# Graph attention on one core: the first row group's second edges as float8, half of each packed exponential and of each normalised row by ScalarE

## The chip, the cores and the metric

The kernel runs on one core of a Trainium2 chip. The metric is device time in microseconds, the median of three runs. The engines are called as in the profile: PE (TensorE, PEld its weight loads), DVE (VectorE), ACT (ScalarE), POOL (GpSimd), SP (SyncE, which issues DMAs). A q behind a name is the engine's queue of DMA issues.

## The reference

One graph attention layer with a residual, on 8192 nodes of 128 features:

```python
h = jnp.maximum(_layernorm(x, axis=-1), 0.0)          # x: (8192, 128) float32
Wh = h @ W                                            # W: (128, 128)
f1, f2 = Wh @ a[:128, 0], Wh @ a[128:, 0]
e = leaky_relu(f1[:, None] + f2[None, :], 0.2)
e = where(adj == 0, -inf, e)                          # adj: (8192, 8192) int32 of 0 and 1
out = x + softmax(e, axis=1) @ Wh
```

## The kernel before

The adjacency matrix is 256 MB of int32, and every entry is read once. Its rows are worked in 16 row groups of 512 rows (four rows to a partition). A row group goes over 16 units of 512 columns, that is 512 nodes. For each unit the entries of the four rows (0 or 1 each, as bytes) are added up into one code per word, PE transposes the codes, ACT unpacks them into marks (`unpack` in the first row group, `take` and `part` later), DVE makes four tiles of weights from the marks and the exponentials of the nodes (`weights`, L987), and PE multiplies these with the nodes' features, high and low halves in float16 (`product`, L476 and L480), into four accumulators. A unit is 16 pairs of such products.

The first row group is the one that matters here. While it runs, the kernel also computes what all row groups need, one group of 512 nodes per unit: the statistics of x on DVE (`statistics`, L913; `inverses` for a batch of groups, with a root by ACT, L776 and L779), the normalised x (`normalise`, into the tile `xn`: one row of four by ACT, L635, three by POOL, L283), its transposes on PE (`x_transposes`, L422) and the relu by ACT (L643), the features on PE (`features`, L440), their copy to SBUF by ACT (`keep`, L649), two small exponentials by ACT (`exponentials`, L675 and L676), their packing into two float16 halves of one word by DVE (`pack`, L965 and L966), the scaled features by POOL (`scaled`, L330), and their high and low float16 parts by ACT and DVE (`high_part`, L764; `low_part`, L974, which ends in `pair_ready`, for which PE waits before it starts a unit).

The order on each engine is written out by hand: each engine walks its own list of these steps and waits on semaphores. In unit b of the first group PE does the first four products' pairs, `features(b+2, 0)`, `x_transposes(b+3)`, four more pairs, `features(b+2, 1)`, four more, the transposes of the codes of unit b+2, and the last four. `x_transposes(g)` waits for ACT's part of `xn` (`xn_ready`) and for POOL's (`xn_pool`). ACT does `high_part(b+1)`, `keep(b+2, 0)`, in some units a root, `second`, `relu(b+3)`, `keep(b+2, 1)`, `exponentials(b+2)`, `unpack(b+2)`, `normalise(b+4)`. POOL does `mix(b+2)`, `normalise(b+4)`, `scaled(b+2)` and then issues loads. DVE does the weights of unit b+1, in some units with `inverses` between their halves (units 2, 5 and 9 among them), `low_part(b+1)`, `pack(b+2)` and the statistics of further groups (`STATS`; group 10 in the loop's third round).

The adjacency of the first row group is loaded by POOL's queue in 16 parts of one unit each (`load_part`, L256; four rows of 512 entries per partition, converted from int32 to bytes on the way), ten of them before POOL's other work and six later (`EARLY`, `PARTS`). The later row groups are loaded in half chunks of two rows of 2048 entries per partition (`load_half`, L291), one half of them to bytes and the other to float8, in which a 1 is the byte 60. For the first group, where all four rows come as plain bytes, ACT multiplies rows 2 and 3 by 200 instead (`second`, L702) before POOL adds them to rows 0 and 1 (`mix`, L274).

x comes by SP's queue in six loads (`LOADS`): groups 0, 1, 2 to 3, 4 to 5, 6 to 9 and 10 to 15, called loads 0 to 5 here. The last three wait until parts 0, 1 and 3 of the adjacency have landed.

## Time and profile before

| | us |
|---|---|
| median of 3 runs (772.83, 772.83, 774.3) | 772.83 |
| the profiled execution | 773.42 |
| its span, first to last instruction | 771.5 |
| PE busy in it | 751.3 (97%) |
| DVE busy in it | 726.5 (94%) |
| ACT busy in it | 579.2 (75%) |
| POOL busy in it | 442.9 (57%) |

The profile is one execution, and all starts and durations below are of it. The busy shares are means over the first row group (up to about 88 us) and the fifteen others, which have different limits, so a change in the first row group is read from that stretch. A timeline row gives the start, the time from the first to the last instruction of the entry, the engine, the line, and in brackets the idle time of the engine before it with what released it.

### The profile page before, as it was taken

What the parts mean: (1) busy time and instruction counts of PE and PEld (TensorE: products, weight loads), DVE (VectorE), ACT (ScalarE), POOL (GpSimd) and SP (SyncE); (2) the same over time, 40 slices, a digit from 0 to 9 for tenths busy, and PEclk for the clock granted to TensorE, in tenths of its full rate; (3) what the DMA queues carried; (4) which work ended last, traced back from release to release, by engine and by line L of the source; (5) the groups of instructions that cost most, each with busy time, mean ns of one, the idle gap of its engine ahead of it and who ended that gap; (6) DMA issues with size and microseconds to landing.
All of it is one profiled execution on the core that took longest, in us unless ns stands there. A gap on an engine that the chain in (4) does not pass through costs nothing.

```text
span 771.5 us, 23891 instructions
## 1 busy us (share of the span) xinstructions
PE 751.3 (97%) x8676; PEld 687.7 (89%) x8676; DVE 726.5 (94%) x1183; ACT 579.2 (75%) x1139; POOL 442.9 (57%) x501
## 2 busy tenths in 40 slices
PE   6899899999999999999999999999999999999997
PEld 5789789999999999999999999999999999999986
DVE  6998899999999999999999999999999999999996
ACT  5889887777778777777877777777777777777762
POOL 8787865646646664664666456465655646564510
PEclk9999999999999999999999999999999999999999
DMA  9999899999999999999999999999999999997100
GB/s 171 179 105 108 85 114 128 108 114 120 107 126 100 116 93 113 108 100 114 97 121 94 118 97 99 112 104 121 90 120 93 99 111 102 115 97 82 19 15 18
DMA packets 48246, 79.70 MB, mean 103 GB/s; under 512 B 2834, under 2 KB 11732, under 8 KB 48212
## 3 DMA queue, kind: packets, MB, share of 16 engines
q0 software_dynamic: 41088, 67.12, 90.5%
q1 hardware_dynamic: 6976, 12.09, 4.6%
q8 instruction: 17, 0.28, 0.1%
q14 instruction: 17, 0.14, 0.1%
q10 hardware_dynamic: 148, 0.07, 0.0%
HBM read 276.37 MB, written 4.23 MB: 364 GB/s over the span
## 4 chain that ended last, share of the span: by engine, by line
PE 91%; DVE 4%; ACT 2%; DMA 1%; POOL 1%; issue 1%; DVEq 0%; ACTq 0%; POOLq 0%
PE acc L476 56%; PE acc L480 29%; PE stage L467 4%; DVE wt_ring L987 2%; PE stage L440 1%; DMA masks<-in_adj_dram 1%; DVE pairs L974 1%; PE stage L422 0%; ACT marks L727 0%; DVE stats L913 0%; PE stage L458 0%; POOL tmp L330 0%; POOL masks L274 0%; DVE xm L1082 0%; ACT wh L649 0%
## 5 line engine op out<-in xcount | busy, mean ns | idle before, releaser
L476 PE MATMUL acc<-pairs,wt_ring 128*128 128x258 f16 x4096 | 717.5, 274 | 4.9 <-DVE pairs L974 3.5
L987 DVE SCALAR_TENSOR_TENSOR wt_ring<-stage,packed,marks 128x512 f32<-128x512 f32 x1024 | 688.4, 744 | 30.9 <-PE acc L480 21.5
L480 PE MATMUL acc<-pairs,wt_ring 128*128 128x129 f16 x4096 | 697.7, 220 | 0.0
L476 PEld LDWEIGHTS acc<-pairs,wt_ring 128*128 128x128 f16 x4096 | 398.8, 98 | 56.2 <-DVE pairs L974 5.1
L480 PEld LDWEIGHTS acc<-pairs,wt_ring 128*128 128x128 f16 x4096 | 400.3, 98 | 4.9
L727 ACT ACTIVATE marks<-codes 128x512 uint16<-128x512 uint8 x480 | 274.6, 620 | 12.5
L717 ACT ACTIVATE codes<-stage 128x512 uint16<-128x512 uint8 x240 | 142.8, 595 | 147.1 <-PE stage L467 146.6
L291 POOL DMA_DIRECT2D masks<-in_adj_dram x120 | 87.7, 731 | 219.8 <-PE stage L467 198.9
L310 POOL TENSOR_TENSOR masks<-masks 128x512 int32<-128x512 int32 x120 | 150.6, 1282 | 1.3
L319 POOL TENSOR_TENSOR masks<-masks 128x256 int32<-128x256 int32 x120 | 87.6, 735 | 55.7 <-ACT masks L710 54.8
L710 ACT ACTIVATE masks<-masks 128x512 uint16<-128x512 uint16 x120 | 74.8, 623 | 1.3 <-POOL masks L310 0.7
L467 PE MATMUL stage<-ident,masks 128*128 128x128 f32 x240 | 67.0, 279 | 0.8 <-ACT codes L717 0.4
L467 PEld LDWEIGHTS stage<-ident,masks 128*128 128x128 f32 x240 | 33.7, 141 | 5.0 <-issue 1.5
L337 POOL TENSOR_SCALAR fin<-fin 128x516 f32<-128x516 f32 x15 | 22.8, 1519 | 2.1 <-ACT fin L752 1.6
L330 POOL TENSOR_TENSOR tmp<-wh,tmp 128x512 f32<-128x512 f32 x16 | 18.0, 1124 | 10.0 <-ACT tmp L676 10.0
L440 PE MATMUL stage<-wx,ht 128*128 128x130 f32 x120 | 20.9, 299 | 1.5 <-ACT ht L643 0.7
L283 POOL TENSOR_SCALAR xn<-xm,small 128x128 f32<-128x128 f32 x42 | 19.4, 471 | 4.3 <-DVE small L937 4.3
L752 ACT ACTIVATE fin<-acc 128x258 f32<-128x258 f32 x60 | 19.4, 381 | 0.0
L347 POOL TENSOR_TENSOR xm<-fin,xm 128x512 f32<-128x512 f32 x15 | 18.0, 1199 | 1.8 <-ACT fin L758 1.5
L758 ACT ACTIVATE fin<-fin,inv 128x128 f32<-128x128 f32 x60 | 19.0, 392 | 0.0
L440 PEld LDWEIGHTS stage<-wx,ht 128*128 128x128 f32 x120 | 16.6, 200 | 2.7 <-ACT ht L643 1.1
L685 ACT ACTIVATE marks<-stage 128x1024 uint16<-128x1024 uint8 x16 | 16.3, 1019 | 1.4 <-PE stage L458 1.4
(78 smaller groups left out, 201.3 us busy)
## 6 DMA issues: line engine op xcount, KB each, us to landing
masks<-in_adj_dram POOLq DMA_DIRECT2D x120, 512.0 KB, 9.7
masks<-in_adj_dram POOLq DMA_DIRECT2D x16, 256.0 KB, 21.9
out_dram<-xm SPq DMA_DIRECT2D x15, 256.0 KB, 7.8
ht<-e_words SPq DMA_DIRECT2D x14, 256.0 KB, 8.5
xm<-in_x_dram SPq DMA_DIRECT2D x1, 1536.0 KB, 13.4
xm<-in_x_dram SPq DMA_DIRECT2D x2, 512.0 KB, 6.6
xm<-in_x_dram SPq DMA_DIRECT2D x1, 1024.0 KB, 9.8
xm<-in_x_dram SPq DMA_DIRECT2D x2, 256.0 KB, 3.1
```

The costliest lines, as they stand in the source:

```text
L291: nc.gpsimd.dma_start(to[:, c * PACK + h:(c + 1) * PACK:2, :], adj_half[q, c, :, h::2, :]).then_inc(adj_second[c] if h else adj_loaded[c], 16)
L310: nc.gpsimd.tensor_tensor(edges4[:, c, :, 0, sl], edges4[:, c, :, 0, sl], edges4[:, c, :, 1, sl], ALU.add).then_inc(s["mixed4"], 1)
L319: nc.gpsimd.tensor_tensor(edges4[:, c, 0, 0, sl], edges4[:, c, 0, 0, sl], edges4[:, c, 1, 0, sl], ALU.add).then_inc(s["joined"], 1)
L337: nc.gpsimd.tensor_scalar(fin[:, :, E1:2 * E1], fin[:, :, E1:2 * E1], 1.0 / LOW, None, ALU.mult).then_inc(s["lows_scaled"], 1)
L440: mm = nc.tensor.matmul(to[:, r * 256:r * 256 + WC], ht[:, g % 2, k:k + P], wx[:], start=(r == 0), stop=(r == 1), skip_group_check=True)
L467: nc.tensor.transpose(stage[:, 0, 0:P], words[:, c * PACK, kk * P:(kk + 1) * P], ident[:]).then_inc(s["transposed"], 1)
L476: return nc.tensor.matmul(acc[:, r, 0:2 * E1], wtv[:, w, r, 1, :], pairv[:, t, :, 0:E1], start=st, stop=end)
L480: return nc.tensor.matmul(acc[:, r, E1:2 * E1], wtv[:, w, r, 0, :], pairv[:, t, 0, 0:E1], start=False, stop=False)
L710: nc.scalar.activation(twos[:, c, 1, 0, sl], twos[:, c, 1, 0, sl], ACT.Copy, scale=2.0).then_inc(s["doubled"], 1)
L717: nc.scalar.activation(codes2[:, b % 2, :].rearrange("p (s w) -> p s w", s=PACK), stage[:, 0, 0:P].bitcast(U8).rearrange("p (w s) -> p s w ...
L727: mm = nc.scalar.activation(split[:, b % MR, :].rearrange("p (s a w) -> p a s w", s=PACK, a=2)[:, h], codes[:, b % 2, :].rearrange("p (s w ...
L987: nc.vector.scalar_tensor_tensor(out=wtq[:, t % NW], in0=e_row, scalar=packed[:, t, 1:2], in1=edges[:, k], op0=ALU.max, op1=ALU.min).then_ ...
```

## The change

Rows 2 and 3 of the first row group are now loaded as float8, so that a 1 arrives as the byte 60, and `second` is gone; `mix` waits for the load alone, and `unpack` scales by 256/60. Each part of the load becomes two transfers, one for rows 0 and 1 and one for rows 2 and 3, on one semaphore that counts to 32. Parts 0 and 1 are still one unit each; the other seven are two units each, with 1024 entries to a row, so that there are 18 transfers in place of 16. Five parts are issued before POOL's other work, one after `scaled(1)`, and one each in the loop's first three rounds. SP's loads 3, 4 and 5 of x now wait for parts 0, 1 and 2, the last of which holds units 2 and 3.

The upper half of the packed exponential, which DVE made from the exponential by a multiplication, is now a third exponential of ACT with another bias, written as float16 between the two others; its constant is a fourth entry of `cst`, and `CUT` is 2 to the power of -16 lower.

ACT now normalises two rows of each group in place of one, and POOL two in place of three; `xn_ready` comes with ACT's second row.

```diff
-CUT = 1.0 - 2.0 ** -11
+CUT = 1.0 - 2.0 ** -11 - 2.0 ** -16
-SECOND = 200.0
-SPLIT = 256.0 / SECOND
+ONE8 = 60.0
+SPLIT = 256.0 / ONE8
-    EARLY = 10
+    EARLY = 5
-    PARTS = {0: (12,), 1: (13,), 2: (14, 15)}
+    PARTS = {0: (6,), 1: (7,), 2: (8,)}
+    UNITS = [(0, 1), (1, 2)] + [(u, u + 2) for u in range(2, UN, 2)]
...
-            for k, part in ((3, 0), (4, 1), (5, 3)):
-                sp.wait_ge(first_loaded[part], 16)
+            for k, part in ((3, 0), (4, 1), (5, 2)):
+                sp.wait_ge(first_loaded[part], 32)
                 load_x(k)
...
-            def load_part(u):
-                c, k = u // KC, u % KC
-                nc.gpsimd.dma_start(masks[:, c * PACK:(c + 1) * PACK, k * BANK:(k + 1) * BANK],
-                                    adj_first[0, u]).then_inc(first_loaded[u], 16)
+            def load_part(k):
+                lo, hi = UNITS[k]
+                c = lo // KC
+                at, to = (lo - c * KC) * BANK, (hi - c * KC) * BANK
+                for h, tiles in ((0, masks), (1, masks8)):
+                    sl = slice(HALF * h, HALF * (h + 1))
+                    nc.gpsimd.dma_start(tiles[:, c * PACK + HALF * h:c * PACK + HALF * (h + 1), at:to],
+                                        adj_first[0, :, sl, lo * BANK:hi * BANK]).then_inc(first_loaded[k], 16)
 
             load_part(0)
-            load_part(1)
...
-            for u in range(2, EARLY):
-                load_part(u)
+            for k in range(1, EARLY):
+                load_part(k)
...
-                pool.wait_ge(first_loaded[u], 16)
-                pool.wait_ge(s["second_ready"], u + 1)
+                pool.wait_ge(first_loaded[part_of(u)], 32)
...
-                for r in range(1, PACK):
+                for r in range(HALF, PACK):
...
             load_part(EARLY)
-            load_part(EARLY + 1)
...
-                for u in PARTS.get(b, ()):
-                    load_part(u)
+                for k in PARTS.get(b, ()):
+                    load_part(k)
...
-                t = g * PACK
-                nc.scalar.activation(xn[:, g % 2, 0:P], xm[:, g, 0:P], ACT.Identity, scale=small[:, 5, t:t + 1],
-                                     bias=small[:, 6, t:t + 1]).then_inc(s["xn_ready"], 1)
+                for r in range(HALF):
+                    t = g * PACK + r
+                    mm = nc.scalar.activation(xn[:, g % 2, r * P:(r + 1) * P], xm[:, g, r * P:(r + 1) * P],
+                                              ACT.Identity, scale=small[:, 5, t:t + 1], bias=small[:, 6, t:t + 1])
+                mm.then_inc(s["xn_ready"], 1)
...
                 nc.scalar.activation(exps, wh[:, sl, Fo:WC], ACT.Exp, scale=1.0 - SLOPE, bias=cst[:, 0:1])
+                nc.scalar.activation(packedv[:, sl, :, 1], wh[:, sl, Fo:WC], ACT.Exp, scale=1.0 - SLOPE,
+                                     bias=cst[:, 3:4])
...
-            def second(b):
-
-                c, k = b // KC, b % KC
-                act.wait_ge(first_loaded[b], 16)
-                sl = slice(k * BANK // 2, (k + 1) * BANK // 2)
-                nc.scalar.activation(twos[:, c, 1, :, sl], twos[:, c, 1, :, sl], ACT.Copy, scale=SECOND
-                                     ).then_inc(s["second_ready"], 1)
...
-                if b + (2 if b == 0 else 3) < UN:
-                    second(b + (2 if b == 0 else 3))
-                elif b >= UN - 2:
+                if b >= UN - 2:
                     double(0, b - UN + 2, b - UN + 3)
...
-                then(nc.vector.tensor_scalar(packedv[:, sl, :, 1], exps, CUT / LOW, None, ALU.mult))
...
+            nc.vector.memset(cst[:, 3:4], float(math.log(SCALE * CUT))).then_inc(s["cst_ready"], 1)
```

## Rows read from the trace of the kernel before

**Rows 1.** Busy time by stages, PE alone: stretch, length, busy (instructions), clock, DMA share, GB/s.
```profile
15.42:30.47 15.05, 10.59 (x95) 1.00 1.16 207
30.47:44.89 14.42, 13.38 (x138) 1.00 1.22 133
44.89:63.00 18.11, 17.54 (x184) 1.00 1.17 106
...
88.70:764.00 675.30, 673.44 (x7938) 1.00 0.95 100
```

**Rows 2.** Timeline of PE: the first products of units 4, 5 and 9.
```profile
39.52 0.29 PE L476 MATMUL acc<-pairs,wt_ring 128*128 128x258 f16 x1 [0.18 <-DVE pairs L974]
...
44.89 0.29 PE L476 MATMUL acc<-pairs,wt_ring 128*128 128x258 f16 x1 [0.86 <-DVE pairs L974]
...
63.01 0.28 PE L476 MATMUL acc<-pairs,wt_ring 128*128 128x258 f16 x1 [0.57 <-DVE pairs L974]
```

**Rows 3.** Loads 4 and 5 of x (line L200): issue, ns, start; then landing.
```profile
L200 SPq DMA_DIRECT2D xm<-in_x_dram x1: 380/380/380, 12.3 to 12.3; - x1
...
DMA to landing us min/median/max: 9.8/9.8/9.8
...
L200 SPq DMA_DIRECT2D xm<-in_x_dram x1: 381/381/381, 21.7 to 21.7; - x1
...
DMA to landing us min/median/max: 13.4/13.4/13.4
```

**Rows 4.** Timeline of DVE: statistics of groups 6, 7 and 9, 10; weights of unit 4.
```profile
23.38 1.42 DVE L913 BATCH_NORM_STATS2 stats<-xm 128x6 f32<-128x256 f32 x4
...
34.79 1.44 DVE L913 BATCH_NORM_STATS2 stats<-xm 128x6 f32<-128x256 f32 x4
36.13 2.72 DVE L987 SCALAR_TENSOR_TENSOR wt_ring<-stage,packed,marks 128x512 f32<-128x512 f32 x4
```

**Rows 5.** DMA by stretches: length, TensorE clock, DMA share, GB/s as written.
```profile
3.00:5.00 2.00, 1.00 1.05 384
...
25.20:33.40 8.20, 1.00 1.12 240
34.00:54.00 20.00, 1.00 1.24 105
126.50:132.50 6.00, 1.00 1.06 165
```

**Rows 6.** Timeline of ACT from the exponentials of group 13 to the next `high_part`.
```profile
75.10 0.27 ACT L675 ACTIVATE stage<-wh,cst 128x8 f32<-128x8 f32 x1
75.31 0.29 ACT L676 ACTIVATE tmp<-wh,cst 128x4 f32<-128x4 f32 x1
75.58 1.02 ACT L685 ACTIVATE marks<-stage 128x1024 uint16<-128x1024 uint8 x1
76.50 0.48 ACT L635 ACTIVATE xn<-xm,small 128x128 f32<-128x128 f32 x1
76.88 0.63 ACT L764 ACTIVATE pairs<-tmp 128x516 f16<-128x516 f32 x1
```

**Rows 7.** Timeline of PE: `x_transposes` of units 11 and 12.
```profile
72.87 0.60 PE L422 MATMUL stage<-ident,xn 128*128 128x128 f32 x4
...
77.22 0.60 PE L422 MATMUL stage<-ident,xn 128*128 128x128 f32 x4
```

**Rows 8.** Groups by line: two with ns min/median/max and starts, two from the page.
```profile
L702 ACT ACTIVATE masks<-masks x16: 613/622/631, 9.8 to 77.7; 128x512 uint16<-128x512 uint16 x16
L965 DVE TENSOR_SCALAR packed<-stage x16: 153/168/171, 10.9 to 84.3; 128x8 f16<-128x8 f32 x16
L283 POOL TENSOR_SCALAR xn<-xm,small 128x128 f32<-128x128 f32 x42 | 19.4, 471 | 4.3 <-DVE small L937 4.3
L291 POOL DMA_DIRECT2D masks<-in_adj_dram x120 | 87.7, 731 | 219.8 <-PE stage L467 198.9
```

**Rows 9.** Timeline of ACT: end of the root of the last batch.
```profile
59.93 0.21 ACT L779 ACTIVATE small<-small 128x16 f32<-128x16 f32 x1
```

More of the change, by code:

```diff
@@ L50 @@
 SCALE = 0.015
-CUT = 1.0 - 2.0 ** -11
+CUT = 1.0 - 2.0 ** -11 - 2.0 ** -16
 TOP = 512.0
 NORM = 1.01
-SECOND = 200.0
-SPLIT = 256.0 / SECOND
+ONE8 = 60.0
+SPLIT = 256.0 / ONE8
 ABOVE = 0.1
-ONE8 = 60.0
 APART = 64.0
@@ L100, in batch_of, with part_of @@
         return next(k for k, (lo, hi) in enumerate(BATCHES) if lo <= g < hi)
+    def part_of(u):
+        return next(k for k, (lo, hi) in enumerate(UNITS) if lo <= u < hi)
     with ExitStack() as ctx:
@@ L128, in gat_kernel @@
         a_row = sb("a_row", [2, P], F32)
-        cst = sb("cst", [P, 3], F32)
+        cst = sb("cst", [P, 4], F32)
         stats = sb("stats", [P, NB, 3], F32)
@@ L149, in gat_kernel @@
             "adj_second0", "adj_second1", "adj_second2", "adj_second3",
-            *(f"first_loaded{u}" for u in range(UN)),
+            *(f"first_loaded{k}" for k in range(len(UNITS))),
             "ident_zero", "ident_ready", "cst_ready", "rows_done", "out_stored", "x_again",
@@ L155, in gat_kernel @@
             "scaled_ready", "high_ready", "pair_ready",
-            "second_ready", "mixed", "marked", "mixed4", "doubled", "joined", "taken", "lows_scaled", "sums_ready", "inv_ready", "fin_scaled", "limits_ready", "limits_turned", "flag_ready",
+            "mixed", "marked", "mixed4", "doubled", "joined", "taken", "lows_scaled", "sums_ready", "inv_ready", "fin_scaled", "limits_ready", "limits_turned", "flag_ready",
             "transposed", "weighted", "spent", "acc_done", "acc_free",
@@ L160, in gat_kernel @@
         adj_second = [s[f"adj_second{c}"] for c in range(NC)]
-        first_loaded = [s[f"first_loaded{k}"] for k in range(UN)]
+        first_loaded = [s[f"first_loaded{k}"] for k in range(len(UNITS))]
         x_loaded = [s[f"x_loaded{k}"] for k in range(len(LOADS))]
@@ L170, in gat_kernel @@
         adj_half = adj.rearrange("(q p s) (c k) -> q c p s k", p=P, s=PACK, k=CHUNK)
-        adj_first = adj.rearrange("(q p s) (b k) -> q b p s k", p=P, s=PACK, k=BANK)
+        adj_first = adj.rearrange("(q p s) k -> q p s k", p=P, s=PACK)
         words = masks.bitcast(F32)
@@ L666, in exponentials @@
                 if g == 0:
-                    act.wait_ge(s["cst_ready"], 3)
+                    act.wait_ge(s["cst_ready"], 4)
                 if g == 0:
@@ L770, in root @@
                 if k == 0:
-                    act.wait_ge(s["cst_ready"], 3)
+                    act.wait_ge(s["cst_ready"], 4)
                 if k == 0:
@@ L793, in _ @@
             root(0)
-            second(0)
             exponentials(0)
@@ L803, in _ @@
             exponentials(1)
-            second(1)
             relu(2)
@@ L827, in _ @@
                     unpack(b + 2, b + 2, first=True)
-                if b == 0:
-                    second(3)
                 if b + 4 < NQ:
```

## The prediction

> **What bounds the kernel now.** I read PE's busy time by stages first, because PE is the busiest engine. From 88.7 us on, PE works 673.4 of 675.3 us [rows 1]. That is the fifteen steady row groups, and the change doesn't touch them. What it can win or lose lies in the first row group, where the same three readings show 4.5, 1.0 and 0.6 us without PE work [rows 1]. Next, in PE's timeline, come the places where it starts again after a pause: units 4, 5 and 9 of the first row group, at 39.52, 44.89 and 63.01 us. Each time the releaser is DVE's `low_part` (L974) [rows 2]. So up to 45 us the first group runs at the pace of DVE, and after that at PE's own pace, 4.35 us for a unit (from one `x_transposes` to the next, 72.87 to 77.22) [rows 7], apart from the pause before unit 9. DVE in turn is almost never idle there, but two of its `statistics` stand close behind a load of x. Load 4 (groups 6 to 9) is issued at 12.3 and lands 9.8 us later, at 22.1; load 5 (groups 10 to 15) is issued at 21.7 and lands at 35.1 [rows 3]. The `statistics` that need them begin at 23.38 and, for group 10, in the second half of the entry at 34.79, so near 35.46 [rows 4]. Load 5 thus has 0.4 us in hand. Last I read the rate of the transfers, since these 60 us are full of them [rows 5].
>
> **What is removed.** Sixteen `second` leave ACT (0.62 us each; a following instruction starts 0.52 after it), sixteen first halves of `pack` leave DVE (0.17 us, some 0.2 with the semaphore behind it), and fourteen `xn` rows leave POOL (0.47 us) [rows 8]. `mix` now waits for its load alone. In units where DVE is the bound this gives 0.2 us a unit; elsewhere it is no time by itself. One unit also has an `inverses` between its weights: unit 5. I take its round to be 0.5 us shorter (0.2 from `pack`, 0.3 from GpSimd standing less in DVE's way; between 0 and 0.8, the pause before unit 5 being 0.86 [rows 2]).
>
> **What is added on POOL.** Eighteen transfers are issued where sixteen were, at 0.73 us each [rows 8], so 1.5 us more of issuing. The eight behind the identity matrix occupy the same time as the eight before. Of the others, one more than before stands behind `scaled` in unit 0 and one in unit 1, where the saved `xn` row pays 0.47 of each. Behind them waits the next `mix`, whose product is needed a unit later: 0, and 0.5 us if that cover is gone (twice 0.73 less 0.47). The float8 conversion I put at 0, because half of the 120 later loads already convert so and all are issued at the same 0.73 [rows 8]; between -0.3 and +0.3 us.
>
> **Transfers: the share of x.** Adjacency rows are read as int32 and written as bytes, so their written rate is a quarter of their read rate. Alone, x runs at 384 GB/s and adjacency writes 105, that is reads 420 [rows 5]. With both running, let x take u and adjacency read v. Then u/384 + v/420 = 1 and u + v/4 is the written rate. At 240 (25.2 to 33.4 us, adjacency in pieces of 512 int32, 2 KB) u is 186 and v 217. At 165 (126.5 to 132.5 us, pieces of 2048 int32, 8 KB, beside the SP queue's store and row load in 2 KB pieces) u is 83 and v 330 [rows 5]. So v/u is 1.17 in the one and 4.0 in the other: for each 2 KB piece of the SP queue about one adjacency piece goes by, however long it is. The change makes the pieces of parts 2 to 8 twice as long, 4 KB. With v/u between 2.0 and 2.34, u falls to 136 to 122 GB/s; I take the middle, 129. Loads 3 and 4 together are 1.57 MB, as is load 5: 8.5 us at 186 become 12.2 at 129, 3.7 more. Load 4 then lands at 25.8. Load 5 used to begin about 3 us after load 4 had landed; now it is queued behind it in time, begins at about 25.3, as before, and lands 3.7 later, at 38.8. (SP waits for units 2 and 3 before it issues load 5; the adjacency gains the share that x loses, so this wait is no later than 21.7.)
>
> The Trainium skill, page "DMA: Bandwidth & Descriptors", section "SWDGE vs HWDGE vs iDMA", says that an engine changes queue only between packets, and that a packet of GpSimd's descriptors is preferably up to 4096 B. Packed so, two 2 KB reads would already have shared a turn before the change, and 4 KB pieces would take nothing more from x. The ratio of 1.17 speaks against it; the case is the second below, with a chance of its own.
>
> **What it costs on DVE.** `statistics(6)` waits for 25.8 in place of 23.38, which throws DVE back by 2.4 us; whatever it wins back of that before group 10, the next wait covers. `statistics(10)` waits for 38.8, 3.3 us after it runs now. Behind it on DVE's queue stand the four weights of unit 4 and `low_part(4)`, and PE waits for that. From the start of these statistics to the weights are 0.67 us, and from there to unit 4 on PE 3.39 (36.13 to 39.52 [rows 2, 4]): unit 4 starts at 38.85 + 4.06 = 42.9, 3.4 later than now. Unit 5 follows 0.5 faster: +2.9 us. With 136 and 122 GB/s it is +2.3 and +3.6.
>
> **What it costs on ACT.** Each unit gains one exponential and one `xn` row and loses one `second`. By busy time that is nearly even (+0.21 +0.38 -0.52), but the three lie in different places. `second` stood ahead of a wait for PE; the added two stand behind it, on a round that closes through PE. The round runs: `x_transposes`, products and `features` on PE, `keep`, exponentials, `unpack`, `normalise` on ACT, and the next `x_transposes`, which needs ACT's part of `xn`. In unit 12 of now, `normalise` starts at 76.50, lasts 0.48, and PE's `x_transposes` follows at 77.22: 0.24 in hand [rows 6, 7]. An exponential takes 0.21 (75.10 to 75.31). `unpack` comes 0.27 after the last exponential, so up to 0.06 of that may be a wait for PE's transposes, in which the new one hides: it adds 0.15 to 0.21, and I take 0.15. One more `xn` row adds 0.38 (76.50 to 76.88) [rows 6]. 0.15 + 0.38 - 0.24 = 0.29 us that PE waits in each unit where it ran without a pause: units 6, 7, 10, 11 and 12 (the pause before 9 takes in that of 8), 1.45 us. The pause before unit 9 hangs on ACT's root of the last batch, which ends at 60.14 [rows 9] behind the same two instructions: +0.5. At the group's end one exponential lies ahead of the last `unpack`: +0.15. Sum +2.1; with 0.2 or 0.35 a unit, 1.65 to 2.4. POOL's smaller half is done earlier and doesn't help, because `x_transposes` waits for both.
>
> **Sum.** +2.9 + 2.1 = +5.0 us. The profiled execution took 773.42 us (span 771.5 and 1.9 around it), so its like would take 778.4. It lies 0.6 above the median of 772.83, so I predict 777.8 for the median.
>
> **The cases.**
> 1. Forecast, both costs: 777.8. Low end 776.5 (+2.3 with 0.3 more gained at unit 5, and +1.65), high end 779.3 (+3.6 with nothing gained there, so 4.1, and +2.4). Chance 0.62.
> 2. x keeps its share, because turns go by bytes up to 4 KB. Load 5 lands at 35.1; DVE, ahead by 0.2 us of `pack` a unit, comes to `statistics(10)` before that and waits; unit 4 comes 0.2 us earlier and, with the 0.5 of its round, unit 5 0.7. ACT's round costs its 2.1: +1.4, 774.2 (773.6 to 774.9). For it: the adjacency's alone rate is the same with 2 KB and 8 KB pieces, so nothing else makes long pieces greedier. Against: the two ratios. Chance 0.18, most of it within 0.2% of no change.
> 3. x loses its share, but ACT's round closes in time, because the 0.24 in hand is larger than I read it: +2.9, 775.7. Chance 0.06.
> 4. The other side: ACT's round closes within PE's 4.35 us and x comes no later. Then the removed `second` and `pack` let DVE run ahead, -0.7 at unit 5 with load 5 at 35.1, 772.1; and if load 5 lands a microsecond earlier, since 1 KB writes might be cheaper, -1.8, 771.0. It is decided at load 5 landing before 34 us and the `xn` part costing under 0.1 beyond the hidden. Chance 0.14, 0.09 of it faster.
>
> About 0.2%, 1.5 us, is what a measurement of this kernel tells from no change. Slower by more: 0.62 + 0.06 + 0.05 of case 2 = 0.73. Within it: 0.13 + 0.05 = 0.18. Faster: 0.09. The range takes in cases 1 to 3, 773.6 to 779.3; that leaves out case 4 and a little above, under 0.2.
>
> **What would show it.** The DMA rate while x loads: 129 GB/s of x and a quarter of 280, near 200 GB/s written in place of 240, for some 24 us without the gap at 22 to 25. DVE idle ahead of `statistics` at about 24 and 37 us, with the x load as releaser. PE idle of some 2.5 us ahead of unit 4, then idle of about 0.3 at L422 in units 6, 7, 10, 11 and 12 with ACT's `xn` (the line of `normalise`) as releaser, and a pause above 1 us before unit 9. If load 5 lands near 35 us, the share step is wrong; if L422 shows no idle, the round step is. The stages after the first group should take the same time to a few tenths.

## The result, and the profile after

The changed kernel takes 781.74 us (median of 4 runs, 780.87 to 782.43) beside 772.88 for the kernel before: a ratio of 1.0108, 95% interval 1.0095 to 1.0120, so 8.9 us slower. I had forecast 777.8 and a range up to 779.3. The sign, the share of x and ACT's round were right, the size was not. The profiled execution took 782.02 us with a span of 778.7, so the span is 7.2 us longer and what lies around it 1.4 us longer (3.3 in place of 1.9).

First, where the 7.2 us are. Line numbers are those of the kernel shown: in the kernel after the products are L481 and L485, `low_part` L967, the statistics L907, the weights L980, `x_transposes` L427. Busy time by stages, PE alone, kernel after (stretch, length, busy, clock, DMA share, GB/s written):

```profile
14.50:37.00 22.50, 15.98 (x133) 0.92 1.09 202
32.00:35.80 3.80, 3.53 (x21) 0.55 1.09 205
38.00:54.00 16.00, 14.46 (x150) 1.00 1.12 107
...
95.80:771.10 675.30, 673.44 (x7938) 1.00 0.95 100
```

The last row is that of the steady groups in [rows 1], moved back by 7.1 us and equal in every digit: all is lost in the first row group. The first row has the 200 GB/s that the argument of the share called for, while x loads; the second is a fall of the granted clock that I had not foreseen.

The places where PE starts again after a pause (timeline of PE: unit 2 in the kernel before, then units 2, 5 and 9 in the kernel after):

```profile
30.47 0.28 PE L476 MATMUL acc<-pairs,wt_ring 128*128 128x258 f16 x1 [1.65 <-DVE pairs L974]
...
32.27 0.40 PE L481 MATMUL acc<-pairs,wt_ring 128*128 128x258 f16 x1 [2.77 <-DVE pairs L967]
...
49.01 0.29 PE L481 MATMUL acc<-pairs,wt_ring 128*128 128x258 f16 x1 [1.32 <-DVE pairs L967]
...
68.94 0.28 PE L481 MATMUL acc<-pairs,wt_ring 128*128 128x258 f16 x1 [1.32 <-DVE pairs L967]
```

Against [rows 2], unit 5 comes 4.12 us later and unit 9 5.93. Before unit 2 PE now waits 2.77 us in place of 1.65; its first products then last 0.40 us in place of 0.28. Unit 4 starts at 42.87 without a pause, 3.35 later than in the kernel before.

The loads of x, kernel after (line L204: loads 4 and 5, issue and landing):

```profile
L204 SPq DMA_DIRECT2D xm<-in_x_dram x1: 380/380/380, 13.1 to 13.1; - x1
...
DMA to landing us min/median/max: 13.6/13.6/13.6
...
L204 SPq DMA_DIRECT2D xm<-in_x_dram x1: 380/380/380, 20.2 to 20.2; - x1
...
DMA to landing us min/median/max: 18.6/18.6/18.6
```

Load 4 lands at 26.7 and load 5 at 38.8; the forecast was 25.8 and 38.8, and [rows 3] have 22.1 and 35.1. What DVE makes of it (timeline of DVE, kernel after):

```profile
18.64 1.43 DVE L907 BATCH_NORM_STATS2 stats<-xm 128x6 f32<-128x256 f32 x4 [1.76 <-DMA xm<-in_x_dram]
...
26.80 1.44 DVE L907 BATCH_NORM_STATS2 stats<-xm 128x6 f32<-128x256 f32 x4 [2.59 <-DMA xm<-in_x_dram]
...
37.90 0.17 DVE L959 SCALAR_TENSOR_TENSOR packed<-packed,stage 128x8 f16<-128x8 f16 x1 [1.71 <-ACT tmp L685]
37.98 1.60 DVE L907 BATCH_NORM_STATS2 stats<-xm 128x6 f32<-128x256 f32 x4
39.50 2.71 DVE L980 SCALAR_TENSOR_TENSOR wt_ring<-stage,packed,marks 128x512 f32<-128x512 f32 x4
```

DVE waits for loads 3 and 4. At group 10 it comes only at 37.98, held up by ACT's exponentials, which are late because unit 2 ran at half the clock (see The clock, below). Its entry is 1.60 us long where it was 1.44 [rows 4]: the second half found load 5 just landed. Two causes thus end at the same place, and by my estimate from these rows either alone would have put the weights of unit 4 near 39.4.

ACT's round, kernel after (timelines of ACT and of PE):

```profile
77.05 0.27 ACT L682 ACTIVATE stage<-wh,cst 128x8 f32<-128x8 f32 x1
77.26 0.29 ACT L683 ACTIVATE packed<-wh,cst 128x8 f16<-128x8 f32 x1
77.45 0.29 ACT L685 ACTIVATE tmp<-wh,cst 128x4 f32<-128x4 f32 x1
77.64 1.00 ACT L694 ACTIVATE marks<-stage 128x1024 uint16<-128x1024 uint8 x1
78.54 0.87 ACT L641 ACTIVATE xn<-xm,small 128x128 f32<-128x128 f32 x2
...
74.76 0.66 PE L427 MATMUL stage<-ident,xn 128*128 128x128 f32 x4
...
79.46 0.66 PE L427 MATMUL stage<-ident,xn 128*128 128x128 f32 x4
```

From one `x_transposes` to the next are 4.70 us, in [rows 7] 4.35. From the first exponential to `unpack` are 0.59 us, in [rows 6] 0.48: the third exponential costs 0.11. `x_transposes` now begins 0.05 us after ACT's last row ends (78.54 and 0.87, then 79.46), where it began 0.24 after it.

### The profile page after: what moved, and what is told of

The parts are those of the page before. It is cut to its first block, busy times and chain, and to the rows that moved or that the text cites. A ratio compares the mean times of both kernels' runs of the same rounds, so it can differ in the third digit from the quotient of the medians.

```text
span 778.7 us, 23862 instructions
## 1 busy us (share of the span) xinstructions
PE 754.2 (97%) x8676; PEld 688.8 (88%) x8676; DVE 725.2 (93%) x1168; ACT 579.1 (74%) x1153; POOL 436.7 (56%) x489
## 4 chain that ended last, share of the span: by engine, by line
PE 89%; ACT 4%; DMA 3%; DVE 1%; issue 1%; POOL 1%; DVEq 0%; ACTq 0%; POOLq 0%
PE acc L481 55%; PE acc L485 28%; PE stage L472 4%; DMA xm<-in_x_dram 2%; ACT marks L694 1%; DMA masks<-in_adj_dram 1%; PE stage L445 1%; PE stage L427 1%; ACT xn L641 1%; ACT wh L656 1%; DVE wt_ring L980 1%; ACT packed L683 0%; ACT marks L727 0%; DVE pairs L967 0%; POOL masks L264 0%
## 5 line engine op out<-in xcount | busy, mean ns | idle before, releaser
L481 PE MATMUL acc<-pairs,wt_ring 128*128 128x258 f16 x4096 | 717.8, 274 | 8.4 <-DVE pairs L967 7.0
L980 DVE SCALAR_TENSOR_TENSOR wt_ring<-stage,packed,marks 128x512 f32<-128x512 f32 x1024 | 688.4, 743 | 31.2 <-PE acc L485 21.6
L485 PE MATMUL acc<-pairs,wt_ring 128*128 128x129 f16 x4096 | 698.0, 220 | 0.0
L481 PEld LDWEIGHTS acc<-pairs,wt_ring 128*128 128x128 f16 x4096 | 398.9, 98 | 59.8 <-DVE pairs L967 8.6
L485 PEld LDWEIGHTS acc<-pairs,wt_ring 128*128 128x128 f16 x4096 | 400.3, 98 | 5.0
L907 DVE BATCH_NORM_STATS2 stats<-xm 128x6 f32<-128x256 f32 x32 | 12.0, 421 | 7.7 <-DMA xm<-in_x_dram 7.6
L656 ACT ACTIVATE wh<-stage 128x260 f32<-128x260 f32 x28 | 10.6, 379 | 10.4 <-PE stage L445 10.4
```

The source lines that it names most:

```text
L481: return nc.tensor.matmul(acc[:, r, 0:2 * E1], wtv[:, w, r, 1, :], pairv[:, t, :, 0:E1], start=st, stop=end)
L485: return nc.tensor.matmul(acc[:, r, E1:2 * E1], wtv[:, w, r, 0, :], pairv[:, t, 0, 0:E1], start=False, stop=False)
L980: nc.vector.scalar_tensor_tensor(out=wtq[:, t % NW], in0=e_row, scalar=packed[:, t, 1:2], in1=edges[:, k], op0=ALU.max, op1=ALU.min).then_ ...
```

## The experiments

All were timed against the kernel before on the same chip. "Outside" is the time of a run less its span (median of the runs), "round" the interval of two `x_transposes` late in the first row group; starts are from the profiled execution.

| kernel | us | ratio (interval) | outside | round | unit 5 | unit 9 |
|---|---|---|---|---|---|---|
| before | 772.88 | 1 | 1.9 to 2.1 | 4.35 | 44.89 | 63.01 |
| after | 781.74 | 1.0108 (1.0095 to 1.0120) | 3.4 | 4.70 | 49.01 | 68.94 |
| e1_rows_back | 777.9 | 1.0052 (1.0036 to 1.0069) | 3.5 | 4.35 | 48.80 | 66.97 |
| e2_short_pieces | 780.27 | 1.0083 (1.0066 to 1.0100) | 3.4 | 4.70 | 47.08 | |
| e3_pairs_only | 777.15 | 1.0043 (1.0030 to 1.0055) | 1.9 | | 49.58 | |
| e4_fill | 781.18 | 1.0098 (1.0081 to 1.0115) | 3.4 | | 47.84 | |
| e5_exp_back | 779.2 | 1.0078 (1.0061 to 1.0095) | 1.9 | 4.60 | 47.96 | 67.52 |
| e6_rows_exp_back | 776.36 | 1.0042 (1.0028 to 1.0056) | 1.9 | 4.35 | 47.32 | 65.43 |
| e7_x_early | 780.54 | 1.0085 (1.0068 to 1.0101) | 3.5 | | 48.03 | |
| e8_rows_back_x_early | 776.56 | 1.0042 (1.0026 to 1.0059) | 3.6 | | 45.28 | 63.46 |
| e9_both_exps | 779.58 | 1.0080 (1.0063 to 1.0097) | 1.8 | 4.70 | 48.13 | 68.05 |
| e10_two_rows_only | 775.94 | 1.0032 (1.0020 to 1.0045) | 1.9 | 4.60 | 45.55 | 65.22 |
| e11_exp_only | 775.5 | 1.0025 (1.0016 to 1.0035) | 3.5 | 4.34 | 44.65 | 62.82 |
| e12_fours | 783.72 | 1.0134 (1.0117 to 1.0151) | 1.8 | 4.35 | 54.94 | 73.05 |
| e13_dve_spare | 778.84 | 1.0059 (1.0040 to 1.0079) | 1.8 | | 47.91 | |
| e14_third_row_spare | 775.0 | 1.0022 (1.0012 to 1.0032) | 2.1 | | | |
| e15_third_row_again | 775.21 | 1.0026 (1.0012 to 1.0039) | 2.1 | 4.60 | 45.51 | 64.48 |

The start of the first row group, the landing of part 0 of the adjacency, varies between executions from 9.1 to 10.7 us, and load 5 of x landed at 37.3 to 38.8 us in the seven kernels that load as the changed one does (after, e1, e4, e5, e6, e9, e13). So differences of less than a microsecond between the starts of two kernels mean little by themselves; intervals inside one execution say more. In time, e1, e5, e9, e12 and e13 came out 0.6 to 2.3 us below the range of the theory that I held, and e2, e8, e10 and e11 0.4 to 1.6 above theirs.

### The loads alone, and the length of the pieces

**e3_pairs_only** is the kernel before with longer pieces and nothing else: parts of two units, nine transfers, bytes as before.

```diff
-    EARLY = 10
+    EARLY = 6
-    PARTS = {0: (12,), 1: (13,), 2: (14, 15)}
+    PARTS = {1: (7,), 2: (8,)}
+    UNITS = [(0, 1), (1, 2)] + [(u, u + 2) for u in range(2, UN, 2)]
...
```

> The kernel before with one edit: the first group's loads come in pieces of 1024 entries (two parts of one unit, seven of two units, nine transfers of four rows, all as bytes); ScalarE's doubling of the second edges, the packing and the normalising are as before. Theory (length of the pieces decides what x gets): load 4 takes about 13.5 us and load 5 about 18.5 us to land, the rate beside x is 200 GB/s, DVE waits ahead of its statistics, and the time is 775.5 to 777.5 us. Rival (float8, or two transfers for a part, makes x late): loads as before, 9.8 and 13.4 us, and 772.5 to 773.5 us.

**e2_short_pieces** is the changed kernel with pieces of 512 entries again, in 32 transfers.

```diff
-    UNITS = [(0, 1), (1, 2)] + [(u, u + 2) for u in range(2, UN, 2)]
+    UNITS = [(u, u + 1) for u in range(UN)]
-    PARTS = {0: (6,), 1: (7,), 2: (8,)}
+    PARTS = {0: (8, 9), 1: (10, 11), 2: (12, 13), 3: (14, 15)}
...
```

> The changed kernel with parts of one unit each, so that the float8 and byte loads come in pieces of 512 entries as before, in 32 transfers. Theory (one adjacency piece goes by for each piece of x, so pieces twice as long halve the share that x gets beside them): load 4 lands about 10 us and load 5 about 13.5 us after issue, the written rate beside x is 240 GB/s again, DVE's waits ahead of statistics shrink from 1.8 and 2.6 us to under 0.7, unit 2 starts by 31 us in place of 32.3, the clock stays at full speed, and the time falls by 2.5 to 4 us to 778 to 779. Rival (x is late because part 0 and part 1 land later and because float8 halves hold up the queue, not for the length of the pieces): loads 4 and 5 still take 13 and 18 us, 781 to 783 us.

**e12_fours** is e3_pairs_only with the suspected cause doubled: six transfers, the last three with pieces of 2048 entries.

```diff
+    UNITS = [(0, 1), (1, 2), (2, 4), (4, 8), (8, 12), (12, 16)]
...
```

> The kernel before, but the first row group's adjacency comes in six transfers of 1, 1, 2, 4, 4 and 4 units, so that the pieces of the last three are 2048 int32 (8 KB) long: the suspected cause doubled once more. Theory of the share (one adjacency piece goes by for each 2 KB piece of x, however long it is): beside 8 KB pieces x moves 83 GB/s, as beside the second row group's store; the written rate beside x is near 165 GB/s, load 4 lands near 31 us and load 5 near 50 us, `statistics` of group 10 waits for it, unit 4 starts near 54 us instead of 39.5, and the time is 786 to 790. Rival (turns go by bytes, and the 129 GB/s beside 4 KB pieces were all there is to lose): load 5 lands near 38.8, 777 to 778.

The rates beside x, PE busy by stretches (one row each of e2_short_pieces, e3_pairs_only and e12_fours, and the end of the adjacency in e12_fours):

```profile
25.00:33.00 8.00, 6.02 (x59) 1.00 1.12 238
...
14.00:36.00 22.00, 16.68 (x145) 1.00 1.09 201
...
20.00:22.00 2.00, 1.48 (x14) 1.00 1.06 166
...
42.00:44.00 2.00, 2.00 (x25) 0.95 0.97 245
```

Pieces of 2, 4 and 8 KB give 238, 201 and 166 GB/s written, whether half of them arrive as float8 or none does. Solved as in the prediction, x gets 183, 132 and 84 GB/s. That is 1.2, 2.1 and 3.9 bytes of adjacency read for each byte of x: for each 2 KB piece of x about one piece of the adjacency goes by, as forecast. The Trainium skill, page "DMA: Bandwidth & Descriptors", section "SWDGE vs HWDGE vs iDMA", has packets of GpSimd's descriptors, preferably of up to 4096 B, as the unit between two turns. If packets were filled so, 2 KB and 4 KB pieces would leave x alike, and here they don't (183 and 132 GB/s).

In e12_fours load 5 landed at 45.3, not at 50: the adjacency was through at about 42 us, after which x had the engines to itself, an end that my sum left out. DVE and PE then (timelines of DVE and PE, e12_fours):

```profile
30.69 1.42 DVE L918 BATCH_NORM_STATS2 stats<-xm 128x6 f32<-128x256 f32 x4 [7.38 <-DMA xm<-in_x_dram]
...
36.24 0.40 PE L481 MATMUL acc<-pairs,wt_ring 128*128 128x258 f16 x1 [7.58 <-DVE pairs L979]
```

The 10.6 us that this kernel loses stand at unit 5, 10.05 us late. e3_pairs_only loses 3.3 us by its ratio, more than the 2.9 of my sum, though it has none of ACT's or POOL's edits; after a pause of 2.62 us before unit 4 its clock was 0.66 in the mean from 43 to 48 us. In e2_short_pieces loads 4 and 5 land 10.1 and 12.9 us after issue and x comes in time (DVE waits 0.33 us in all), but four issues stand in a row on POOL for 2.94 us in each of the first rounds, `mix` comes late, and PE waits 1.45 us for it shortly before unit 5, which starts 1.93 us earlier than in the kernel after and still 2.19 later than in the kernel before. It shows the share by its rate and its landings; its time, above what I expected, mixes that with what the issues cost on POOL.

**e6_rows_exp_back** is the changed kernel with both of ACT's additions taken back: what is left is the loads and the missing `second`.

```diff
-                for r in range(HALF, PACK):
+                for r in range(1, PACK):
-                for r in range(HALF):
+                for r in range(1):
-                nc.scalar.activation(packedv[:, sl, :, 1], wh[:, sl, Fo:WC], ACT.Exp, scale=1.0 - SLOPE,
-                                     bias=cst[:, 3:4])
+                then(nc.vector.tensor_scalar(packedv[:, sl, :, 1], exps, CUT / LOW, None, ALU.mult))
```

> The changed kernel with both moves of work undone: x normalised one row by ScalarE and three by GpSimd, and the upper exponential half by VectorE. What is left of the change are the loads (float8 halves, 18 transfers, pieces of 1024 entries) and the missing doubling on ScalarE. Theory: no idle at x_transposes, the late loads of x remain (13.5 and 18.5 us), and in the span +3 to +4.5 us against the kernel before, as pairs alone gave; 776.5 to 778 us with what lies around the span. Rival (the doubling that is gone gives back what the loads cost): 773 to 774.5 us. If the 1.4 us outside the span stay, they belong to the loads.

Timelines of DVE and PE, e6_rows_exp_back:

```profile
37.80 0.77 DVE L905 BATCH_NORM_STATS2 stats<-xm 128x6 f32<-128x256 f32 x2 [1.24 <-DMA xm<-in_x_dram]
...
42.25 0.28 PE L481 MATMUL acc<-pairs,wt_ring 128*128 128x258 f16 x1 [1.90 <-DVE pairs L966]
47.32 0.29 PE L481 MATMUL acc<-pairs,wt_ring 128*128 128x258 f16 x1 [0.56 <-DVE pairs L966]
```

Here the chain is the predicted one, link by link: DVE waits for load 5, unit 4 is 2.73 us late, unit 5 gains 0.30 of it back, and from there to unit 9 are 18.11 us as before (18.12). So at unit 5 the load term is 2.4 us where ACT and POOL are left alone; I had 2.9. (By its ratio e6 loses 3.2 us; its profiled execution is 0.7 us faster than its median.)

**e7_x_early** and **e8_rows_back_x_early** issue loads 3 and 4 of x at about 8 us and load 5 at about 13, in the changed kernel and in e1_rows_back.

```diff
-            for k, part in ((3, 0), (4, 1), (5, 2)):
-                sp.wait_ge(first_loaded[part], 32)
-                load_x(k)
+            sp.wait_ge(s["ht_ready"], 1)
+            load_x(3)
+            load_x(4)
+            sp.wait_ge(first_loaded[1], 32)
+            load_x(5)
```

> The changed kernel with the last three loads of x issued earlier: loads 3 and 4 when the first relu is done (7.5 us) and load 5 when part 1 has landed (13 us), in place of parts 0, 1 and 2. Theory (DVE's waits for x delay units 2 to 5, ACT's round the rest): loads 3, 4 and 5 land near 15, 23 and 36 us, DVE no longer waits ahead of its statistics, unit 2 starts by 30 us without a pause of 2.8 and with the clock at full speed, unit 5 comes 2 to 3.5 us earlier, but the period of 4.70 us bites in more units (2 to 4 as well), which takes back about 1 us: 779 to 780.5 us. Rival (adjacency is what lacks, and x earlier makes it later): mix waits for parts 1 and 2 and the time stays at 781 to 783.

> Both causes removed: x loads issued earlier as in the run before this one, and x normalised one row by ScalarE and three by GpSimd; float8 loads, the missing doubling and ScalarE's third exponential stay. Theory: no idle at x_transposes and no wait for x, so the span comes to 770 to 772 us, at or a little under the kernel before (771.5); with the 1.4 us outside the span 773.5 to 775. Rival (a third cause in the span is left): 776 us or more.

The waits for loads 3 and 4 shrink (e7_x_early: 0.44 and 1.68 us), but load 5 still lands at 37.2, since its share is what it was. The ratios fall from 1.0108 to 1.0085 and from 1.0052 to 1.0042, with overlapping intervals. Neither beats the kernel before. e8's 776.56 is above the 775 that I allowed: with both causes lessened 3.2 us by the ratio are left, 1.6 of them outside the span. In its profiled execution 0.39 of the rest stand at unit 5 and 0.54 at the end of the first row group; I can't say what they are.

### The clock

**e4_fill** adds twenty products that nobody reads behind unit 1, so that PE doesn't rest before unit 2.

```diff
+                if b == 1:
+                    for k in range(20):
+                        nc.tensor.matmul(acc[:, 2, 300:300 + P], ident[:], ident[:], start=False, stop=False,
+                                         skip_group_check=True)
```

> The changed kernel with 20 products of the identity matrix, into columns that nothing reads, on PE behind unit 1, where PE stands still for 2.8 us before unit 2 and the granted clock then is 0.5 for 3.8 us. Theory: with PE at work the clock stays at 1.0, unit 2 is 1.5 us shorter, but DVE then stands before the statistics of group 10 until load 5 of x has landed at 38.8 us, so that unit 4 starts at 42.7 as it does now and the time falls by 0.0 to 0.4 us. Rival (the low clock is itself the cost): unit 4 and the end come 1.5 us earlier, 780.2 us.

The stretch that had a clock of 0.55 in the kernel after (PE busy by stretches, e4_fill):

```profile
32.00:35.80 3.80, 3.80 (x41) 1.00 1.09 204
```

With PE at work before unit 2 the granted clock stays at 1.00, 2.4 GHz; in the kernel after, back from its rest of 2.77 us, PE ran at 0.50, 1.2 GHz, and took 5.85 us for unit 2 in place of 4.36. But the run doesn't price the low clock (timelines of DVE and PE, e4_fill):

```profile
30.11 0.69 DVE L971 SCALAR_TENSOR_TENSOR pairs<-pairs,tmp 128x516 f16<-128x516 f16 x1
...
36.74 0.17 DVE L963 SCALAR_TENSOR_TENSOR packed<-packed,stage 128x8 f16<-128x8 f16 x1 [1.97 <-ACT tmp L689]
...
32.62 0.27 PE L481 MATMUL acc<-pairs,wt_ring 128*128 128x258 f16 x1
```

`low_part` is done at 30.80, but the fill occupies PE until 32.6. So it holds unit 2 back by 1.8 us, about what the clock would have cost, and DVE waits for ACT's exponentials as it does in the kernel after (1.97 and 1.71 us). That the time hardly falls (1.0098 in place of 1.0108, within the intervals) therefore decides between neither theory nor rival.

What decides is an execution in which unit 2 ran at the full clock without a fill, that of e13_dve_spare (described below, one idle DVE instruction more per group). Its clock was at 0.50 earlier, from 26 to 28 us, and at 1.00 from 30 us on; unit 2 starts at 31.54 (timelines of DVE and PE):

```profile
37.97 0.77 DVE L909 BATCH_NORM_STATS2 stats<-xm 128x6 f32<-128x256 f32 x2 [1.26 <-DMA xm<-in_x_dram]
...
42.07 0.29 PE L483 MATMUL acc<-pairs,wt_ring 128*128 128x258 f16 x1 [1.32 <-DVE pairs L970]
```

From the start of unit 2 to the end of ACT's exponentials are 4.10 us here and 5.60 in the kernel after: the half clock is what made them late. Here DVE doesn't wait for them, but 1.26 us for load 5, which lands at 38.0, and unit 4 starts 4.07 us after that landing, as in the kernel after (38.8 and 42.87). So load 5 alone would have put unit 4 where it is, and the low clock cost next to nothing there.

### ACT's round

**e1_rows_back** gives POOL its third row back (the first four lines of e6_rows_exp_back's diff); **e5_exp_back** only undoes the exponential (its other lines).

> The changed kernel with x normalised as before, one row by ScalarE and three by GpSimd. Theory (ACT's round through PE is too long by 0.35 us in every unit without a pause, and the pause before unit 9 grows with it): the idle of about 0.3 at x_transposes in units 3, 6, 7, 8, 10, 11 and 12 goes, the pause before unit 9 falls from 1.3 to about 0.9; the first row group ends 2.3 to 3 us earlier, 779 us. The late loads of x stay late (4 and 5 land 13.6 and 18.6 us after issue). Rival (everything comes from the late loads of x, and ACT's longer round only fills pauses): 781.7 us, no change.

> The changed kernel with the upper half of the packed exponential made by VectorE again, so that ScalarE issues two exponentials a unit. Theory (ACT's round: 0.35 us too long a unit, of which the exponential is 0.15 to 0.2 and the row of x the rest): PE's idle at x_transposes falls to 0.15 to 0.2 a unit, the period from 4.70 to 4.50, and the first row group ends 1.0 to 1.5 us earlier; DVE's extra 0.2 a unit costs nothing, since it is not the last. The loads of x as in the changed kernel. 780.3 to 780.9 us. Rival (DVE is what the first units hang on): unit 2 and unit 5 start 0.4 to 0.8 us later and the time is 781.5 to 782.5. Also open: 1.4 us of the change lie outside the span (3.4 us around it, 2.0 in the kernel before and with pairs only); if they belong to this exponential, they go too.

**e10_two_rows_only** and **e11_exp_only** put one of the two alone into the kernel before, with `second` and all loads as they were.

```diff
-                for r in range(1, PACK):
+                for r in range(HALF, PACK):
-                t = g * PACK
+                for r in range(HALF):
+                    t = g * PACK + r
...
```

> The kernel before with the x rows split two and two alone: one more `xn` row on ScalarE, one less on GpSimd, `second` and all loads as they were. My theory of ScalarE's round, with the sizes measured since: a row of 0.38 us on a round that has about 0.2 us in hand where `second` still stands ahead of it, so `x_transposes` waits 0.15 to 0.2 us in some seven units and a little at unit 9: 774 to 775.5, with 1.7 to 2.1 us outside the span. Rival 1 (the round has the whole 0.38 in hand as long as the exponential isn't there): no pause at `x_transposes`, 772.5 to 773.3. Rival 2 (the row costs its whole 0.38 in every unit, as in the changed kernel): 776 to 777.

```diff
+                nc.scalar.activation(packedv[:, sl, :, 1], wh[:, sl, Fo:WC], ACT.Exp, scale=1.0 - SLOPE,
+                                     bias=cst[:, 3:4])
...
-                then(nc.vector.tensor_scalar(packedv[:, sl, :, 1], exps, CUT / LOW, None, ALU.mult))
...
```

> The kernel before with the third exponential on ScalarE alone: VectorE's first instruction of `pack` is gone, everything else as before. My theory: 0.15 to 0.2 us more on ScalarE's round fits into the 0.2 it has in hand, and VectorE's saving of 0.2 a unit brings unit 5 up to 0.7 us earlier, so the span is 770.8 to 771.7; but the run is 3.3 to 3.7 us longer than its span, so 774 to 775. Rival 1 (what lies outside the span has nothing to do with this instruction): 1.7 to 2.1 us outside, 772.2 to 773. Rival 2 (the exponential breaks the round): a pause at `x_transposes` of 0.1 to 0.2 us a unit, and 1 us more on top of either.

The round is 4.35 with neither (before, e6) and 4.34 to 4.35 with the exponential alone (e11, e1), 4.60 with the second row alone (e10, e5), 4.70 with both. Each of the three pairs has one kernel with `second` and one without, so its removal gives the round nothing. A second row of 0.38 costs 0.25, and the 0.11 of the exponential is free until the row is there, then costs 0.10: about 0.13 were in hand, not 0.24. e10 lost more than I expected of it (775.94, not 774 to 775.5), for a reason of its own, next. e1 gained more than I expected of it: 4.3 us by the ratios, 3.05 of them at the start of the second row group in the profiled executions. e5 gained 2.3 us by the ratios, of which 1.5 lie outside the span.

### POOL before VectorE

In units 5 and 9 `low_part` (L967) is long. POOL's `normalise` and `scaled` and DVE's `low_part` ahead of unit 9 (timelines, kernel after):

```profile
66.36 0.88 POOL L289 TENSOR_SCALAR xn<-xm,small 128x128 f32<-128x128 f32 x2 [1.24 <-DVE small L931]
67.28 1.05 POOL L336 TENSOR_TENSOR tmp<-wh,tmp 128x512 f32<-128x512 f32 x1
...
67.49 1.39 DVE L967 SCALAR_TENSOR_TENSOR pairs<-pairs,tmp 128x516 f16<-128x516 f16 x1
```

and the same in the kernel before:

```profile
61.09 1.31 POOL L283 TENSOR_SCALAR xn<-xm,small 128x128 f32<-128x128 f32 x3 [0.98 <-DVE small L937]
62.37 1.48 POOL L330 TENSOR_TENSOR tmp<-wh,tmp 128x512 f32<-128x512 f32 x1
...
62.21 0.73 DVE L974 SCALAR_TENSOR_TENSOR pairs<-pairs,tmp 128x516 f16<-128x516 f16 x1
```

Of the two, the one that begins second is the longer: `scaled` 1.48 in place of 1.05, or `low_part` 1.39 in place of 0.73. With one row less POOL comes 0.2 us ahead of DVE, and the lengthening falls on the one that PE waits for. In all eight kernels in which POOL does three rows `low_part` takes 0.72 or 0.73 us in units 5 and 9, and in all eight with two rows 1.31 to 1.50 (e14's profile left out). **e14_third_row_spare**, run again as **e15_third_row_again**, is e10_two_rows_only with the third row back on POOL, into a spare tile. (The rows are of the second; its expectation says why.)

```diff
-                for r in range(HALF, PACK):
+                for r in range(1, PACK):
-                    ins = nc.gpsimd.tensor_scalar(xn[:, g % 2, r * P:(r + 1) * P], ...
+                    ins = nc.gpsimd.tensor_scalar(spare[:, g % 2, :] if r == 1 else xn[:, g % 2, r * P:(r + 1) * P], ...
```

> The kernel before with ScalarE doing two of the four x rows, and GpSimd still doing three, the first of them into a spare tile that nothing reads. Beside the kernel in which GpSimd does only two (775.94 us) it tells what GpSimd's shorter work does by itself. Theory: with two rows GpSimd reaches `scaled` 0.2 us before VectorE reaches `low_part` of units 5 and 9, and `low_part` then takes 1.42 us in place of 0.73; with the third row back `scaled` comes second again, `low_part` takes 0.7 in both units, and units 5 and 9 start 0.6 to 0.7 us earlier each: 774.4 to 774.9. The pause of `x_transposes` of 0.25 us a unit stays. Rival: `low_part` is long because of what ScalarE's second row does to VectorE's round; then nothing changes, 775.5 to 776.4.

> The same kernel as the one with GpSimd's third row thrown away, whose profiled execution ran at a granted clock of 0.657 and so can't be compared by its rows. In a profile at full clock: by the theory VectorE's `low_part` of units 5 and 9 takes about 0.7 us and `scaled` begins after it, and the pauses of TensorE before units 5 and 9 are 0.6 to 0.7 us shorter than the 1.35 us of the kernel with two rows on GpSimd; the interval between two `x_transposes` stays 4.60 us. By the rival `low_part` takes 1.4 us and the pauses are 1.35 us.

Ahead of unit 9, e15_third_row_again (timelines of POOL, DVE and PE):

```profile
63.86 1.48 POOL L331 TENSOR_TENSOR tmp<-wh,tmp 128x512 f32<-128x512 f32 x1
...
63.70 0.72 DVE L977 SCALAR_TENSOR_TENSOR pairs<-pairs,tmp 128x516 f16<-128x516 f16 x1
...
64.48 0.28 PE L477 MATMUL acc<-pairs,wt_ring 128*128 128x258 f16 x1 [0.66 <-DVE pairs L977]
```

The pause is 0.66 in place of the 1.35 of e10_two_rows_only, and 0.68 in place of 1.35 before unit 5, while the round stays 4.60. (Unit 5 starts no earlier in the table because the whole of this execution began later: from unit 2 to unit 5 are 14.39 us, in e10 15.06.) Work that nobody needs on POOL makes the kernel faster than without it: the ratio falls from 1.0032 to 1.0022 and 1.0026 (the intervals overlap, so it is the pauses that show it, not the times). The Trainium skill, page "SBUF — State Buffer", section "Summary: rules for kernel authors", says that when a VectorE instruction has two SBUF inputs and a GpSimd one reads SBUF, the second to be issued is blocked until the first ends. These rows agree in kind; the second is longer by 0.66 and 0.43 us, while the first still had 0.84 and 0.57 us to go.

### Outside the span

**e9_both_exps** has both instructions, the changed kernel's third exponential of ACT going to a spare tile; **e13_dve_spare** is the same with DVE's result thrown away and ACT's used.

```diff
-                nc.scalar.activation(packedv[:, sl, :, 1], wh[:, sl, Fo:WC], ACT.Exp, scale=1.0 - SLOPE,
+                nc.scalar.activation(sparev[:, sl, :, 1], wh[:, sl, Fo:WC], ACT.Exp, scale=1.0 - SLOPE,
+                then(nc.vector.tensor_scalar(packedv[:, sl, :, 1], exps, CUT / LOW, None, ALU.mult))
```

> The changed kernel, but ScalarE writes its third exponential to a spare tile that nothing reads, and VectorE's first instruction of `pack` is back and fills the upper half. So both instructions are there: it tells to which of the two the 1.4 us outside the span belong. Theory 1 (they go with ScalarE's third exponential): the profiled run is 3.3 to 3.7 us longer than its span, as in the changed kernel; with 0.2 us more for each pack of VectorE's start up to unit 5, the time is 782 to 783. Theory 2 (they go with the instruction that VectorE no longer issues): 1.7 to 2.1 us outside the span, and 780.5 to 781.5. ScalarE's round stays near 4.70 us a unit in both.

```diff
+                then(nc.vector.tensor_scalar(sparev[:, sl, :, 1], exps, CUT / LOW, None, ALU.mult))
```

> The changed kernel with one VectorE instruction more per group: the first instruction of `pack` is back but writes to a spare tile that nothing reads, while ScalarE's third exponential fills the upper half as in the changed kernel. With the kernel whose third exponential went to the spare tile, and whose run was 1.7 us longer than its span, this tells what the 1.4 us more outside the span go with. Theory 1 (the sixteen instructions that VectorE no longer issues): 1.6 to 2.1 us outside, 779.4 to 780.5. Theory 2 (which engine writes the upper half): 3.2 to 3.8 us outside, 781 to 782.

The engines' busy time and instructions (page of the kernel after, then of e13_dve_spare):

```profile
PE 754.2 (97%) x8676; PEld 688.8 (88%) x8676; DVE 725.2 (93%) x1168; ACT 579.1 (74%) x1153; POOL 436.7 (56%) x489
...
PE 752.8 (97%) x8676; PEld 687.2 (88%) x8676; DVE 727.3 (94%) x1184; ACT 578.9 (74%) x1153; POOL 436.2 (56%) x489
```

Sixteen more instructions on DVE, of no use, take the time outside the span from 3.4 back to 1.8. All seven kernels with 1168 instructions on DVE have 3.4 to 3.6 there, all ten with 1183 or 1184, the kernel before among them, have 1.8 to 2.1, and ACT's count (1123 to 1155) has no say. The sixteen instructions that the change saves cost about 1.5 us where no trace reaches. The two groups always differ by the same instruction, the first of `pack`, so whether its kind or the number matters isn't shown, and why fewer cost more stays open. (By the medians the span of e13_dve_spare is 1.3 us shorter as well, that of e9_both_exps 0.5. In the profiled executions the difference, 1.10 and 0.88 us, lies before unit 5, where load 5 landed 0.8 and 1.2 us earlier.)

## Why the prediction was right or wrong

Against the profiled execution I forecast 778.4 and got 782.02, 3.6 us more: 1.3 in unit 5's round, 0.9 in ACT's round and 1.4 outside the span.

**The share of x: right.** 129 GB/s were forecast beside 4 KB pieces; the rate of e3_pairs_only makes it 132, and between the landings of loads 4 and 5 in the kernel after lie 12.1 us for 1.57 MB, 130 GB/s. The pieces alone do it (e3), more length does more (e12), and case 2 is out, and with it case 4, which wanted x no later; the round of 4.70 us puts out case 3. That load 5 landed at 38.8 and unit 4 came 3.35 us late, where 38.8 and 3.4 were forecast, is partly luck: in this execution load 4 was issued 0.8 us later than in [rows 3]. Where it was issued at 12.4 (e13), load 5 landed at 38.0, and in e6, with 37.8, unit 4 came 2.73 us late.

**"The next wait covers": right, but by little.** I let the wait for load 4 vanish behind load 5 and left out the one for load 3. Together they put unit 2 back by 1.8 us, and PE's rest then cost the clock and 1.5 us more, which brought ACT's exponentials nearly as late as load 5. Load 5 still covers it (e13). A sum that lets a stall be covered must ask what the stall does on the way.

**Unit 5's round: wrong in sign, 1.3 us.** I took 0.5 off, 0.2 for `pack` and 0.3 for GpSimd standing less in DVE's way; the round was 0.77 longer (5.37 to 6.14). Timeline of DVE, kernel after, in `inverses` and at `low_part`:

```profile
45.52 0.18 DVE L924 TENSOR_TENSOR small<-small 128x16 f32<-128x16 f32 x1 [0.26 <-ACT small L779]
...
47.56 1.39 DVE L967 SCALAR_TENSOR_TENSOR pairs<-pairs,tmp 128x516 f16<-128x516 f16 x1
```

0.66 of it is `low_part`. POOL's row was costed at "done earlier and doesn't help", but being done earlier puts `scaled` ahead of `low_part` (e15). The rest is `inverses`: 1.35 us in place of 1.16, since DVE waits 0.26 us there for ACT's root. Where it doesn't wait (e6) `inverses` takes 0.86 and the whole round is 0.30 shorter, so the 0.3 was there to be had. Of the 0.2 for `pack` 0.12 came.

**ACT's round: right mechanism, mis-sized, 0.9 us.** After unit 5 I forecast +2.1 and 2.97 came (row group 1 starts 7.09 late, unit 5 4.12). A unit costs 0.35, not 0.29: the exponential 0.11 in place of 0.15, but the 0.24 in hand was really 0.13 (e10). 0.05 of the difference is the gap that is left even where PE waits for ACT; the other 0.06 stays open. It bites six times where I counted five, 2.1 us. Before unit 9 I had 0.5 for ACT's root; the pause grew by 0.75, 0.66 of it `low_part`. The end of the group cost 0.1.

**Outside the span: not in the sum, 1.4 us.** I carried its 1.9 over as a constant, and it was not one (e13).

**No time elsewhere: right.** The fifteen other row groups are unchanged, and POOL's issues and the float8 conversion show no cost of their own: with both e6 has 1.0042, without them e3 has 1.0043.

The parts add up: by the ratios the loads cost 0.42% (e6), the rows 0.32% (e10) and the exponential with its 1.5 us outside 0.25% (e11), together 0.99% of the 1.08%, each with an interval of about 0.1 to 0.14 to either side. They aren't independent: taken out of the changed kernel the rows give back 0.56% (e1), the exponential 0.30% (e5) and the two together 0.66% (e6).

## What to carry to other kernels

Two queues with pieces of different length didn't share by bytes here: before pieces are made longer to save transfers, work out what the transfer beside them has left, from the rates at two lengths. Work taken from an engine off the path can cost time on it, when that engine then comes first to something that it shares with the one on the path: look who begins first now, and by how much. What a round has in hand can be less than the gap that a timeline shows, here 0.13 us of 0.24: try it with the added work alone before you build on it. And before an experiment is read, look whether its own edit is in the way: the fill that kept the clock up held back the very unit that it was to speed up.

## What was unexpected of the hardware

- The time outside the span was 3.4 to 3.6 us in the kernels with 1168 instructions on VectorE and 1.8 to 2.1 in those with 1183 or 1184, whether the sixteen more did anything or not.
- VectorE's `low_part` took 0.73 us when it began before GpSimd's `scaled` and 1.39 when it began 0.2 us after; `scaled` took 1.48 or 1.05.
- TensorE's clock fell to 1.2 GHz after a rest of 2.77 us and was back at 2.4 GHz some 4 us later, with the engine at work. After e12_fours' rest of 7.58 us it was low from 32 to 42 us. The length of the last rest alone doesn't foretell it: it was at 0.50 from 32 to 34 us in e7_x_early after a rest of 1.88 us, and stayed at 1.00 in e3_pairs_only after one of 2.48.
